# Three softmax-type reciprocals moved from VectorE to one Ln and Exp on ScalarE, with input normalisation and masks rearranged on GpSimd

## What is computed

```python
xn = layernorm(x)
q, k, v = split(xn @ Wqkv.T + bqkv)             # 16 heads of 8
q, k = layernorm(q)*g_q + b_q, layernorm(k)*g_k + b_k
aw = softmax(q @ k.T / sqrt(8))                 # 256 x 256 for each head
kth = top_k(aw, 12)[..., -1:]                   # the 12th largest of each row
aws = aw * (aw >= kth)
o_s = (aws / (aws.sum(-1) + 1e-8)) @ v          # reciprocal 1
qf, kf = softmax(q, -1), softmax(k, -1)         # over the 8 of a head: reciprocal 2 (kf)
z = qf . kf.sum(tokens)
o_l = (qf @ (kf.T @ v)) / (z + 1e-6)            # reciprocal 3
o = sigmoid(alpha)*o_s + (1 - sigmoid(alpha))*o_l
y = x + o @ Wproj.T + bproj + (xn @ W[idx] + b[idx])
```

## Time and profile before

| | |
|---|---|
| median of 3 runs | 1214.25 us (1212.27 to 1215.47) |
| profiled execution, its own time | 1203.79 us |
| span of the profiled execution | 1202.0 us |
| granted TensorE clock, mean | 0.99 |
| DVE busy | 1164.2 us, 97% |
| ACT busy | 1094.4 us, 91% |
| POOL busy | 1090.9 us, 91% |
| PE busy | 951.5 us, 79% |

### The profile page before, as it was taken

The page is one execution under the profiler, slowest core; times in us unless marked ns, Lnnn a source line. Parts: engine busy times, 40 slices in busy tenths (PEclk is TensorE's granted clock), DMA queues, the critical chain, the costliest instruction groups (busy, mean ns, idle before and its releaser), DMA issues.

```text
span 1202.0 us, 34514 instructions
## 1 busy us (share of the span) xinstructions
PE 951.5 (79%) x9028; PEld 647.2 (54%) x9028; DVE 1164.2 (97%) x4448; ACT 1094.4 (91%) x3566; POOL 1090.9 (91%) x1691
## 2 busy tenths in 40 slices
PE   4578788887788788788788787888888788787786
PEld 1355555555555555555555555555555555555554
DVE  6999999999999999999999999999999999999993
ACT  3699999999999999999999998999999999999984
POOL 5699999999999999999999999999999999999974
PEclk9999999999999999999999999999999999999998
DMA  3122222122222122222122222122222121222210
GB/s 102 41 63 67 86 84 72 49 70 65 85 85 80 42 75 59 85 85 85 38 74 59 85 85 84 40 73 59 85 85 85 46 67 58 85 81 80 58 34 14
DMA packets 165126, 82.77 MB, mean 69 GB/s; under 512 B 7737, under 2 KB 164927, under 8 KB 164930
## 3 DMA queue, kind: packets, MB, share of 16 engines
q1 hardware_dynamic: 164658, 80.43, 23.4%
q10 hardware_dynamic: 272, 0.13, 0.0%
HBM read 42.78 MB, written 37.75 MB: 67 GB/s over the span
## 4 chain that ended last, share of the span: by engine, by line
ACT 33%; DVE 28%; issue 19%; PE 9%; POOL 8%; DVEq 2%; DMA 0%; POOLq 0%; ACTq 0%
ACT e L821 19%; DVE rest L646 11%; DVE top L639 10%; POOL below L440 6%; ACT kept L788 4%; DVE next L652 4%; PE pv_ps L964 3%; PE work_ps L1030 2%; ACT below L834 2%; DVEq L75 2%; ACT e L826 1%; PE turn_ps L943 1%; ACT osT L793 1%; ACT oT L843 1%; ACT xnT L882 1%
## 5 line engine op out<-in xcount | busy, mean ns | idle before, releaser
L440 POOL TENSOR_SCALAR below<-e,next 128x256 bf16<-128x256 f32 x768 | 695.8, 922 | 0.0
L821 ACT ACTIVATE e<-score_ps,drop 128x256 f32<-128x256 f32 x1024 | 475.1, 493 | 42.8 <-POOL drop L410 39.7
L646 DVE MATCH_REPLACE8 rest<-e 128x256 f32<-128x256 f32 x1024 | 416.7, 411 | 0.1
L652 DVE MAX8 next<-rest 128x8 f32<-128x256 f32 x1024 | 409.4, 413 | 0.3
L943 PE MATMUL turn_ps<-ident,e 128*128 128x128 f32 x2048 | 388.4, 284 | 15.7 <-ACT kept L788 15.7
L944 PE MATMUL turn_ps<-minus_huge,below 128*128 128x128 bf16 x2048 | 367.8, 221 | 0.0
L639 DVE MAX8 top<-score_ps 128x8 f32<-128x256 f32 x1024 | 361.0, 417 | 3.3 <-PE score_ps L925 3.1
L943 PEld LDWEIGHTS turn_ps<-ident,e 128*128 128x128 f32 x2048 | 290.7, 142 | 67.2 <-issue 33.1
L788 ACT ACTIVATE kept<-turn_ps 128x1024 f32<-128x1024 f32 x256 | 272.1, 1063 | 23.3 <-PE turn_ps L944 23.1
L821 ACT ACTIVATION_READ_ACCUMULATOR e<-score_ps,drop 128x1 f32 x1024 | 230.9, 226 | 0.0
L944 PEld LDWEIGHTS turn_ps<-minus_huge,below 128*128 128x128 bf16 x2048 | 218.6, 107 | 0.7
(11 more groups left out here) (176 smaller groups left out, 1346.2 us busy)
## 6 DMA issues: line engine op xcount, KB each, us to landing
part_slots<-part SPq DMA_DIRECT2D x128, 192.0 KB, 2.3
q_slots<-part_slots SPq DMA_DIRECT2D x64, 256.0 KB, 3.5
k_slots<-part_slots SPq DMA_DIRECT2D x64, 256.0 KB, 3.9
part_slots<-part SPq DMA_DIRECT2D x64, 128.0 KB, 1.9
x_sb<-in_L_attn_x SPq DMA_DIRECT2D x32, 128.0 KB, 4.1
x_res<-in_L_attn_x SPq DMA_DIRECT2D x32, 128.0 KB, 4.1
out_y<-out_sb SPq DMA_DIRECT2D x32, 128.0 KB, 4.3
w_ops<-in_L_ffn_W SPq DMA_DIRECT2D x1, 512.0 KB
```

Source lines behind the costliest of these rows:

```text
L440: nc.gpsimd.tensor_scalar(below[:, r, t, :], e[:, r, t, :], next8[:, r, t, TOPK - 9:TOPK - 8], None, ALU.is_lt).then_inc(s["below_pool"], 1)
L646: nc.vector.match_replace(rest[:, t, :], e8[:, (u_ - 1) % 2, t, :], e[:, (u_ - 1) % RING, t, :], REMOVED).then_inc(s["rest_ready"], 1)
L652: nc.vector.max(next8[:, (u_ - 1) % RING, t, :], rest[:, t, :]).then_inc(s["next_ready"], 1)
L821: nc.scalar.activation(e[:, u_ % RING, t, :], score_ps[:, u_ % 2, t // 2, t % 2, :], ACT.Exp, bias=drop[:, u_ % 2, t, 0:1], accum_out=z[:, ...
```

## The change

- The three reciprocals leave DVE. The three operands (`sums_sb`, `lin_raw`, `k_sum`) become parts of one tile `over`; in unit 6 ACT takes the logarithm of all 96 columns at once, in unit 7 it takes `exp(-log)`. POOL's `lin` moves from unit 4 to unit 0 of the next iteration, `k_feat` stands ahead of `o_sparse` in unit 7, and all three wait for the one Exp.
- `den` on POOL (two instructions) goes; the small epsilon is added on PE by two matmuls at the end of `sums`.
- `xn` moves from ACT (unit 5) to POOL (unit 4, after the masks); `shift` moves ahead of the masks of unit 4. In iteration -2 `xn` stays on ACT.
- A mask on POOL becomes two steps: `gap = next8 - e` by one instruction for each tile (bf16 out), then one instruction for all 3 or 4 tiles of the unit that clamps `gap` between 0 and 2^40. POOL makes 25 of a batch's 32 masks (3, 3, 3, 3, 4, 3, 3, 3) where it made 24 (3, 2, 4, 3, 4, 3, 3, 2); ACT makes 7 where it made 8.
- The value products of two neighbouring quads go to the two halves of `pv_ps`, and ACT copies both at once (128x512, units 0 and 4) in place of four copies of 128x256.
- `sums` multiplies by a `gather` of 36 columns where it had 128.

```diff
-POOL_TILES = (3, 2, 4, 3, 4, 3, 3, 2)
+POOL_TILES = (3, 3, 3, 3, 4, 3, 3, 3)
@@ POOL
-                    if u_ == 6 and exists(it - 1):
-                        wait_alone(pool, s["sums_copied"], it, s["waits_passed"])
-                        nc.gpsimd.tensor_scalar(den[:, 0], z[:, nxt].rearrange("p t h -> p (t h)"), SUM_EPS, None,
-                                                ALU.mult).then_inc(s["den_step"], 1)
...
+                    if u_ == 4 and it >= -1 and exists(it + 2):
+                        shift(it)
...
-                        for t in range(POOL_TILES[r]):
-                            wait_alone(pool, s["next_ready"], TILES * (g - 2) + t + 1, s["waits_passed"])
-                            nc.gpsimd.tensor_scalar(below[:, r, t, :], e[:, r, t, :],
-                                                    next8[:, r, t, TOPK - 9:TOPK - 8], None,
-                                                    ALU.is_lt).then_inc(s["below_pool"], 1)
+                        half, many = u_ % 2, POOL_TILES[r]
+                        for t in range(many):
+                            pool.wait_ge(s["next_ready"], TILES * (g - 2) + t + 1)
+                            nc.gpsimd.tensor_scalar(gap[:, half, t, :], e[:, r, t, :], -1.0,
+                                                    next8[:, r, t, TOPK - 9:TOPK - 8], ALU.mult,
+                                                    ALU.add).then_inc(s["gap_step"], 1)
+                        pool.wait_ge(s["gap_step"], POOL_SUM * ((g - 2) // UNITS) + POOL_UPTO[r + 1])
+                        nc.gpsimd.tensor_scalar(below[:, r, 0:many], gap[:, half, 0:many], HUGE, 0.0, ALU.min,
+                                                ALU.max).then_inc(s["below_pool"], many)
...
+                    if u_ == 0 and exists(it - 1):
+                        pool.wait_ge(s["over_ready"], it + 1)
+                        nc.gpsimd.tensor_tensor(lin[:, nxt]..., lin_raw[:, :, 0:D], lin_rec..., ALU.mult)
...
+                    if u_ == 4 and it >= -1 and exists(it + 2):
+                        pool.wait_ge(s["newton"], STEPS * (it + 3))
+                        wait(pool, s["w_xT"], it + 3)
+                        for t in range(NT):
+                            nc.gpsimd.tensor_scalar(xn[:, t], x_sb[:, par, t], rsqrt[:, 3, GROUPS + t:GROUPS + t + 1],
+                                                    x_shift[:, 1, t:t + 1], ALU.mult, ALU.add).then_inc(s["xn_ready"], 1)
@@ DVE
-                    if u_ == 4 and k == 1 and exists(it):
-                        dve.wait_ge(s["lin_copied"], it + 1)
-                        nc.vector.reciprocal(lin_z[:], lin_raw[:, :, D]).then_inc(s["linz_ready"], 1)
-                    if u_ == 7 and k == 1 and exists(it - 1):
-                        dve.wait_ge(s["den_ready"], it)
-                        nc.vector.reciprocal(den[:, 2], den[:, 1]).then_inc(s["rden_ready"], 1)
-                    if u_ == 6 and exists(it + 1) and k == 5:
-                        dve.wait_ge(s["ksum_ready"], it + 2)
-                        nc.vector.reciprocal(k_rec[:], k_sum[:]).then_inc(s["krec_ready"], 1)
@@ ACT
+                    if u_ == 7 and it >= -1 and (exists(it + 1) or exists(it) or exists(it - 1)):
+                        wait(act, s["lin_ready"], it)
+                        act.wait_ge(s["over_logs"], it + 2)
+                        nc.scalar.activation(over_rec[:, lo:hi], over_log[:, lo:hi], ACT.Exp, scale=-1.0).then_inc(
+                            s["over_ready"], 1)
...
-                    if u_ % 2 == 0 and exists(it if u_ >= 6 else it - 1):
+                    if u_ in (0, 4) and exists(it - 1):
...
-                        nc.scalar.copy(oT[:, par if u_ >= 6 else nxt, (u_ - 6) // 2 % 4], pv_ps[:, 0:N]).then_inc(
+                        nc.scalar.copy(oT[:, nxt, u_ // 4].rearrange("p a n -> p (a n)"), pv_ps[:]).then_inc(
...
+                    if u_ == 6 and it >= -1 and (exists(it + 1) or exists(it) or exists(it - 1)):
+                        if exists(it + 1):
+                            act.wait_ge(s["ksum_ready"], it + 2)
+                        if exists(it):
+                            act.wait_ge(s["lin_copied"], it + 1)
+                        if exists(it - 1):
+                            act.wait_ge(s["sums_copied"], it)
+                        nc.scalar.activation(over_log[:, lo:hi], over[:, lo:hi, D], ACT.Ln).then_inc(
+                            s["over_logs"], 1)
@@ PE, sums()
-                            last = nc.tensor.transpose(pv_ps[:, at:at + P], oT[:, nxt, q, t * P:(t + 1) * P], gather[:])
+                            mm(pv_ps[:, at:at + 4 * VA], oT[:, nxt, q // 2, 1 - q % 2, t * P:(t + 1) * P], gather[:],
+                               start=(t == 0 and q == 0), stop=False, skip_group_check=True)
...
+                        last = mm(over_t, eps_ident[:], z[:, nxt, t, :], start=False, stop=True, skip_group_check=True)
```

More of the change, by code:

```diff
@@ L172, in build @@
         qfT = sb("qfT", [P, N])
-        lin_raw = sb("lin_raw", [P, NT * H, VA])
-        lin_z = sb("lin_z", [P, NT * H])
+        over = sb("over", [P, 3 * NT * H, VA])
+        over_log = sb("over_log", [P, 3 * NT * H])
+        over_rec = sb("over_rec", [P, 3 * NT * H])
+        sums_sb, lin_raw = over[:, 0:NT * H], over[:, NT * H:2 * NT * H]
+        k_sum = over[:, 2 * NT * H:, D]
+        sums_rec, lin_rec, k_rec = (over_rec[:, i * NT * H:(i + 1) * NT * H] for i in range(3))
         lin = sb("lin", [P, 2, NT, C])
@@ L184, in build @@
         e = sb("e", [P, RING, TILES, N])
+        gap = sb("gap", [P, 2, TILES, N], BF16)
         below = sb("below", [P, RING, TILES, N], BF16)
@@ L187, in build @@
         z = sb("z", [P, 2, NT, H])
-        oT = sb("oT", [P, 2, QUADS, N])
-        sums_sb = sb("sums_sb", [P, NT * H, VA])
-        den = sb("den", [P, 3, NT * H])
+        oT = sb("oT", [P, 2, QUADS // 2, 2, N])
         o_sparse = sb("o_sparse", [P, NT, C])
@@ L472, in body @@
                             src = dst
[L473 to L479 removed]
                     if u_ == 7 and exists(it + 1):
[L482 removed]
+                        pool.wait_ge(s["over_ready"], it + 2)
                         pool.wait_ge(s["dexp_ready"], it + 2)
@@ L775, in rsqrt_steps, with over_range @@
                                      scale=float(0.5 ** 0.5)).then_inc(s["rsqrt_ready"], 1)
+            def over_range(it):
+                first = 0 if exists(it - 1) else 1 if exists(it) else 2
+                last = 3 if exists(it + 1) else 2 if exists(it) else 1
+                return first * NT * H, last * NT * H
             def body(it, par, xr):
@@ L798, in body @@
                         wait(act, s["lin_ready"], it)
-                        nc.scalar.copy(lin_raw[:].rearrange("p g e -> p (g e)"), work_ps[:, 0:NT * H * VA]).then_inc(
+                        nc.scalar.copy(lin_raw.rearrange("p g e -> p (g e)"), work_ps[:, 0:NT * H * VA]).then_inc(
                             s["lin_copied"], 1)
@@ L849, in body @@
                         wait(act, s["osp_ready"], it - 1)
-                        nc.scalar.copy(sums_sb[:].rearrange("p g e -> p (g e)"), pv_ps[:, 0:NT * H * VA]).then_inc(
+                        nc.scalar.copy(sums_sb.rearrange("p g e -> p (g e)"), pv_ps[:, 0:NT * H * VA]).then_inc(
                             s["sums_copied"], 1)
@@ L871, in body @@
                             s["y_ready"], 1)
-                    if u_ == 5 and exists(it + 2):
-                        act.wait_ge(s["newton"], STEPS * (it + 3))
-                        wait(act, s["w_xT"], it + 3)
+                    if u_ == 5 and it == -2:
+                        act.wait_ge(s["newton"], STEPS)
+                        act.wait_ge(s["w_xT"], 1)
                         for t in range(NT):
@@ L951, in product @@
                     q = (u_ - 6) // 2 % 4
+                    half = 1 - q % 2
                     pe.wait_ge(s["turn_copied"], 2 * (quad + 1))
-                    wait(pe, s["pv_copied"], quad)
+                    wait(pe, s["pv_copied"], quad // 2)
                     if u_ == 6:
```

70 lines of the change are left out of this document (33 added, 37 removed).

## The result

The changed kernel takes 1226.01 us (median of 4 runs, 1225.49 to 1226.97); the kernel before, in runs beside it, 1214.86 (1212.27 to 1217.22). The ratio is 1.0104, with a 95% interval of 1.0084 to 1.0125. The forecast was 1187 us, a range of 1180 to 1246, and a chance of 0.73 that the kernel gets faster by more than 0.3%. The measured time lies in the range, but on the side that had 0.21, and that side rested on a slow POOL (rivals B and C), which did not come: that the range holds it is luck. The profiled execution took 1226.97 us.

The account below looks back on a forecast made before the run. DVE was taken as the bound. Savings of 20.7 + 5.0 + 0.7 + 0.3 = 26.7 us off 1202.0 gave 1175.3, or 1177.1 profiled; scaled by 1.0087, 1187 us, range 1180 to 1246.

Parts of the forecast that it names:

- rivals B and C: POOL too slow: B at the middle price, 1234 to 1258 us, chance 0.12; C at one-step price, about 1393, 0.11.
- What bounds: Whole kernel: DVE, busy 97%, sets the pace at 35.76 us a batch; ACT and POOL have slack.
- Reciprocals off DVE: DVE's units 4 and 6, start and tail: each reciprocal costs DVE 0.22 us; 94 of them save 20.7 us.
- the stall: Unit 7: DVE's removal waits 0.17 us for ACT's `e8`; expected to go, saving 5.0 us.
- it was preceded and is followed by lighter units: ACT's unit 4: becomes heaviest, with one mask (0.50 us) and 0.25 of copy more; lighter units stand around it.
- `sums` gets shorter ... nothing on the pace waits for this.: PE: shorter `sums`, two small matmuls replace `den`; PE at 79% busy, no cost on the pace.
- D: Unit 7: DVE waits for `e8` instead of computing reciprocals; 1203 to 1214 us, say 1209; chance 0.10.
- The clock: Whole kernel: profiled 1203.79 us beside a median of 1214.25 gave a factor of 1.0087, applied to the forecast.
- POOL: Two-step masks at the low price, 0.77 ns a column: 16.3 us a batch, 5.4 less; POOL 28.3 us.
- the break-even of 22.9: POOL's masks: above 22.9 us a batch, or 1.29 ns a column, POOL would become the bound.
- ACT's sum: ACT, a batch: work removed less Ln and Exp added, net -0.8 to -0.9 us, giving 33.1.
- Start and tail: Start: no wait for `k_sum`, 0.7 us saved; tail: Ln and Exp path 0.3 us shorter, bounded by 1 either way.

Follow-up runs that it names:

- e8: Not a run but a name in the kernel's code: the step of ACT whose end DVE's removal in unit 7 waits for.
- the second profile: The kernel before, unchanged, profiled again: 1213.5 us at a mean clock of 0.963.

## Why the prediction was wrong, step by step

1. **What bounds.** Right: DVE set the pace. It still does in clean batches of the good variants (units of 4.20 us).
2. **Reciprocals off DVE, 20.7 us, and the stall.** Right when done alone: unit 4 and unit 6 fell from 4.41 and 4.42 to 4.21 us, and unit 7 from 4.58 to 4.26. That this kernel takes 1187.3 us, the very time forecast, is luck in part: its clean batch is 35.20 us, not 34.93, and its profiled execution took 1187.08 us where the forecast had 1177.1. It makes up for this by having three low batches where the kernel before usually has 16. In the whole change the first part held (units 4 and 6 at 4.20), but the stall did not go: 4.76 - 4.20 = 0.56 us a clean batch, 0.39 more than the 0.17 that was to vanish. The prediction had seen unit 4's extra mask and copy and passed over them with "it was preceded and is followed by lighter units". ACT's own time did not matter there; the chain from it through PE's shared `pv_ps` did.
3. **PE.** The failed step, with the stall of step 2 beside it. "`sums` gets shorter ... nothing on the pace waits for this." It got longer, from 1.09 us to 2.41, from 8 records to 20, and with it came falls of the clock in unit 5 that make the next scores late: 23 us of the kernel. That a plain fp32 matmul leaves two records stood in the trace of before: `w_v` (L1030) is called twice a batch and counted 128 times, not 64. The Trainium skill (Perfetto Trace Analysis, section on transposes) says to keep a logical transpose a transpose and not a standard matmul; it speaks against this edit, and the traces agree by these numbers (1.98 us for the 8 products, 1.09 for the 8 transposes); the prediction did not weigh it. No rival had a lower clock in it: D had the right wait (DVE at `e8`, 15.2 us) but priced it at most at the old pace.
4. **The clock.** The profiled execution of before had a clock of 0.99 and was 10.5 us short of the median. The prediction scaled by 1.0087 and did not ask what the 10.5 us were. They were low batches (3 against 16 in the second profile, which took 1213.5 us), a cost that the experiments moved either way.
5. **POOL.** Right, at the low end: 482 and 827 ns where 391 and 785 were expected, 1041 for 980; `xn` was mis-sized, 452 for 290. Masks cost (374.0 + 185.3 + 33.3)/32 = 18.5 us a batch, under the break-even of 22.9, and POOL fell from 91 to 82% busy. B and C did not come. From 768 to 1024 columns the clamp adds 214 ns, 0.84 ns a column. The Trainium skill (GPSIMD Engine Reference, section on elementwise work) gives 1.8 cycles an element for a tight loop at best, an estimate of 1.5 ns at its clock; the measured clamp is faster.
6. **ACT's sum.** Right: 1068.0 busy for 1094.4, a drop of 0.83 us a batch for the 0.8 to 0.9 forecast, though no gain came of it.
7. **Start and tail.** The first score maximum came 0.43 us earlier (31.02 for 31.45 in the earlier trace rows; 0.7 forecast). From the end of the sums' copy to `o_sparse` it now takes 0.70 us for the 1.30 of the earlier trace rows, better than forecast. But the tail grew: from DVE's last score maximum to the end 31.1 us for 28.3, since ACT now waits 3.81 us for `sums`, not 1.18.

The sum, for the profiled executions of the change (1226.97) and of the reciprocals alone (1187.08), 39.9 us apart: batches 1 to 29 differ by 34.7. Of this 13.4 is what clean batches alone would give (29 x 35.83, their mean, less the other's 1025.7), and 21.2 the 18 low ones, 18 x (37.01 - 35.83). Most of the rest, 2.9, is the tail.

**What stays open.** Why the clock falls. It is shown that the fall stands where PE's burst stands and that undoing `sums` removes most falls; but the kernel before had a higher clock than its usual one with the 8 products alone, and with the two-step masks alone. Whether it is the amount of PE's work in a stretch or where its pauses lie was not separated. A kernel with the new `sums` and an added pause of PE was not tried.

## What to carry over

Count what an edit does to PE in records of the trace, not in calls or columns: a plain fp32 matmul in place of a transpose was two for one. Where two executions of one kernel differ by 10 us, find what differs before scaling; here it was the clock, the very term that the change moved. And an engine's slack in the mean doesn't cover a delay just ahead of a buffer that another engine shares: follow what waits for it, two units on if need be. (Here that was ACT's copies ahead of PE's value product.)

## What the runs showed that was not expected

- A plain fp32 matmul leaves two MATMUL and two LDWEIGHTS records, and 36 moving columns (284 ns) take no less than 128 of a transpose (280 ns); the transpose leaves one of each.
- At the granted level of 1.2 GHz a turn step starts every 0.32 us, for 0.17, and the value product takes 1.59 us, for 1.07. In the changed kernel most batches with such a stretch took 36.8 us, for 35.6; with the fall in unit 1 of another kernel a batch lost nothing (35.0 to 35.3, for 35.36).
- The mean clock of one kernel's profiled executions was 0.99 once and 0.963 another time, with 3 and 16 low batches of 29, and 1203.8 and 1213.5 us.
- Ln and Exp of 96 columns take 387 and 316 ns by their records, but the instruction behind starts 0.26 and 0.17 us after their own start: together 0.43 us of ACT, half the 0.8 to 0.9 forecast.
